# A decoder layer on one core: in its second mixing stage the four normalisations of a half stand a slot later, with one identity tile for all stages and a reordered head of the first mixing stage

## The chip, the cores and the metric

The kernel runs on one core of one Trainium2 chip. The metric is the device time of one execution in microseconds (us), as the median of three runs. Before the change it is 3562.73 us (3561.97 to 3564.03).

## The reference

Shapes are B=4 sequences of T=1024 tokens with D=512 features. Three residual blocks follow one another, each fed with a row-wise layer normalisation of x:

```python
x = x + attention(layernorm(x))             # 16 heads of 32, ALiBi distances, @ Wout + bout
x = x + mixing(layernorm(x), ctx_1024)      # below
x = x + conv_ffn(layernorm(x))              # quantised 512 -> 2048, 3-tap convolution, 2048 -> 512

def mixing(x, ctx):
    emb = x + ctx
    q, k, v = emb @ wq + bq, emb @ wk + bk, emb @ wv + bv
    ek, ew = exp(k - max_k), exp(w - max_w)             # w: pos_bias, kept within 128 of the diagonal
    y = sigmoid(q) * (ew @ (ek * v)) / (ew @ ek)
    a = layernorm(y @ wo + bo + emb) * gamma + beta
    ff = relu(a @ w1 + b1) @ w2 + b2
    return layernorm(ff + a) * gamma + beta
```

The output must be float32 of shape 4x1024x512.

## The kernel before

Six stages run one after the other, each a function with its own tiles, its own semaphores and a block in which every engine has its own program: `project_qkv`, `attend`, `mix_in` (the first mixing stage), `mix_out` (the second), `cross_ffn`, `quantised_ffn`. Between two stages all engines meet at a barrier. What one stage hands to the next goes through DRAM. A float32 product is done as three products of a high part (`_hi`, rounded by ScalarE) and a low part (`_lo`, the difference, by VectorE or GpSimd). All order is written out by hand; nothing is planned by a program. An engine works its list in order, so one that waits holds everything that stands behind it. Each stage builds its own identity tile `ident` on GpSimd (`identity`, L95: a memset and a select) for TensorE's transposes, and TensorE waits for it with `pe.wait_ge(ident_step, 2)`.

**attend.** 16 turns (a sequence by a group of four heads), each of 32 units. GpSimd starts with an iota (L662), VectorE makes `neg_distance` of it (L851), and GpSimd multiplies it into `bias_table` (L685), one head after the other; VectorE's maximum of the first unit (L863) needs the first of them. SyncE loads the stacked q and k of the turn (L649), then v.

**mix_in.** It works on eight halves of 512 tokens. Its head prepares four weights, `NAMES = ("out", "k", "v", "q")`, through the raw buffers `w_raw` (a view of `kT`): SyncE loads, `round_w` on ScalarE (L1240) rounds, `split_w` on VectorE (L1294) subtracts. The head then does, for half 0: `out_products` on TensorE (L1160, 48 matmuls of 512 columns on `o_in`), `bias_x` on GpSimd (L1113), `residual_norm` on VectorE (L1305 adds, L1307 statistics, L1311 and L113 to L118 the root, L1317 four normalisations), `embed` on GpSimd (L1121 adds the context, L1125 the bias), and TensorE's `turn` (L1189), which transposes the result. After that `step` runs for each half. In the head GpSimd and VectorE wait for all five bias vectors first, and VectorE splits the weights "out" and "k" before `residual_norm(0)`.

**mix_out.** It works on sequences b of eight tiles of 128 tokens; a *slot* s of the loop handles tile s. In the slot, TensorE does in this order: `turn_y(s-2)` (L1622), `turn_e` of a tile ahead (L1604), `weigh` for "den" (L1637 with the sums, then L1643) and for "num", `turn_e` again, and `out_product` of tile s-2 (L1666, 12 matmuls). VectorE does: `split_y(s-2)` (L1747), which `out_product` waits for; `divide(s)` (L1755, L1758, L1761); `residual(s-3)` (L1773 reads the bank of `out_product`, L1775 takes statistics). When `residual` ends a half of four tiles (slots 6 and 2), VectorE adds there the aggregation (L1780), the root (L113 to L118, fourteen small instructions) and four normalisations of 128x512 (L1787). GpSimd's `scale_and_shift` (L1559, L1561) waits for these (`norm_ready`) and stands in slots 7 and 0 for the first half, 3 and 4 for the second, behind its own `split_e` (L1551) of those slots.

There are four banks `acc`. Which one a product takes is fixed by `bank_of` and `free_bank`, and "den" of slot s takes the bank that "out" used two slots earlier:

```python
at = len(KINDS) * s + KINDS.index(kind)
back = at - ACC
before, step = KINDS[back % len(KINDS)], back // len(KINDS)
past(pe, read[before], b * TB + step - (LAG if before == "out" else 0) + 1)
```

With three kinds, `ACC` 4 and `LAG` 2 this makes "den" of slot s wait until L1773 has read output tile s-4, which VectorE does in slot s-1.

## Time and profile before

| | us |
|---|---|
| median of three runs | 3562.73 |
| the profiled execution, its device time | 3561.91 |
| its span, first to last instruction | 3560.3 |
| TensorE busy | 3177.0 (89%) |
| VectorE busy | 2358.0 (66%) |
| ScalarE busy | 1769.2 (50%) |
| GpSimd busy | 1127.6 (32%) |

Stages in time, by the first instructions of each: `attend` from 345.6, `mix_in` from 1477.4, `mix_out` from 1936.0, `cross_ffn` from 2296.6, `quantised_ffn` from about 3100. TensorE is busy nearly all the time within the stages, and idle in their heads. In the timeline a row gives start, duration, engine, line, operation, and in square brackets the idle time of the engine before it with what ended it. PE is TensorE, DVE VectorE, ACT ScalarE, POOL GpSimd, SP SyncE; an engine's name with q is its queue issuing a transfer.

### The profile page before, as it was taken

What the parts mean: (1) busy time and instruction counts of PE and PEld (TensorE: products, weight loads), DVE (VectorE), ACT (ScalarE), POOL (GpSimd) and SP (SyncE); (2) the same over time, 40 slices, a digit from 0 to 9 for tenths busy, and PEclk for the clock granted to TensorE, in tenths of its full rate; (3) what the DMA queues carried; (4) which work ended last, traced back from release to release, by engine and by line L of the source; (5) the groups of instructions that cost most, each with busy time, mean ns of one, the idle gap of its engine ahead of it and who ended that gap; (6) DMA issues with size and microseconds to landing.
All of it is one profiled execution on the core that took longest, in us unless ns stands there. A gap on an engine that the chain in (4) does not pass through costs nothing. (4 is left out here: it accounts for less than half of the span.)

```text
span 3560.3 us, 57155 instructions
## 1 busy us (share of the span) xinstructions
PE 3177.0 (89%) x19234; PEld 2286.5 (64%) x19234; DVE 2358.0 (66%) x4214; ACT 1769.2 (50%) x3131; POOL 1127.6 (32%) x892
## 2 busy tenths in 40 slices
PE   6998999999999999689996898599999999467887
PEld 5776666666666666467775777477887888334443
DVE  5562888888888888555553788634445444379996
ACT  3331888888888888412222222132222222066662
POOL 2343222311321231143331355311111111058886
PEclk9999999999999999889997999799999999689999
DMA  6775212211311222355644443321111110201112
GB/s 216 242 244 166 67 57 74 77 60 56 91 60 57 69 80 64 123 188 187 226 167 155 135 142 124 101 95 42 42 42 43 42 41 30 80 23 54 60 42 71
DMA packets 239608, 350.54 MB, mean 98 GB/s; under 512 B 31792, under 2 KB 129104, under 8 KB 239440
## 3 DMA queue, kind: packets, MB, share of 16 engines
q1 hardware_dynamic: 208784, 291.46, 25.3%
q0 software_dynamic: 8640, 31.77, 2.7%
q10 hardware_dynamic: 22016, 25.17, 2.0%
q8 instruction: 93, 1.52, 0.2%
q14 instruction: 75, 0.61, 0.1%
HBM read 210.68 MB, written 137.64 MB: 98 GB/s over the span
## 5 line engine op out<-in xcount | busy, mean ns | idle before, releaser
L863 DVE CUSTOM_DVE_ANT_0 attend_scores<-attend_scores,attend_bias_table 128x1024 f32<-128x1024 f32 x512 | 630.4, 1231 | 164.0 <-PE attend_scores L717 157.7
L790 ACT ACTIVATE attend_probs<-attend_scores,attend_neg_max 128x1024 f32<-128x1024 f32 x512 | 571.2, 1116 | 136.9 <-DVE attend_neg_max L863 126.8
L729 PE MATMUL attend_turned<-attend_ident,attend_probs 128*128 128x128 f32 x4096 | 557.5, 275 | 11.5 <-DVE attend_probsT L871 11.2
L729 PEld LDWEIGHTS attend_turned<-attend_ident,attend_probs 128*128 128x128 f32 x4096 | 473.0, 141 | 121.4 <-DVE attend_probsT L871 27.2
L717 PE MATMUL attend_scores<-attend_k_stack,attend_q_stack 96*128 96x512 f32 x1024 | 375.2, 448 | 14.4 <-DMA attend_q_stack<-qk_parts 9.8
L798 ACT COPY attend_probsT<-attend_turned 128x512 f32<-128x512 f32 x640 | 359.1, 583 | 25.4 <-PE attend_turned L729 23.5
L2207 DVE TENSOR_TENSOR cross_ffn_h_lo<-cross_ffn_hidden,cross_ffn_h_hi 128x512 fp32r<-128x512 f32 x128 | 96.3, 757 | 361.9 <-ACT cross_ffn_h_hi L2104 361.3
L691 POOL TENSOR_TENSOR attend_out_parts<-attend_out_full,attend_out_parts 128x256 fp32r<-128x256 f32 x64 | 46.5, 727 | 856.7 <-ACT attend_out_parts L805 856.7
L744 PE MATMUL attend_out_acc<-attend_probsT,attend_v_in 128*32 128x256 f32 x4096 | 312.9, 389 | 0.7 <-DVE attend_out_full L881 0.7
L871 DVE COPY attend_probsT<-attend_turned 128x512 f32<-128x512 f32 x384 | 263.4, 686 | 1.3 <-PE attend_turned L729 1.3
L717 PEld LDWEIGHTS attend_scores<-attend_k_stack,attend_q_stack 96*128 96x128 f32 x1024 | 154.1, 190 | 171.4 <-issue 169.2
L2101 ACT ACTIVATE cross_ffn_hidden<-cross_ffn_h_acc,cross_ffn_b_cols 128x512 f32<-128x512 f32 x128 | 88.1, 688 | 264.5 <-PE cross_ffn_h_acc L2018 248.5
L685 POOL TENSOR_TENSOR attend_bias_table<-attend_neg_distance,attend_slope_now 128x1920 f32<-128x1920 f32 x64 | 214.8, 3386 | 1.4 <-POOL attend_slope_now L677 0.2
L2029 PE MATMUL cross_ffn_out_acc<-cross_ffn_w_hi,cross_ffn_h_hi 128*128 128x512 f32 x512 | 206.5, 403 | 1.1 <-DVE cross_ffn_h_lo L2207 0.4
L2016 PE MATMUL cross_ffn_h_acc<-cross_ffn_aT_hi,cross_ffn_w_hi 128*128 128x512 f32 x512 | 202.8, 396 | 5.0 <-issue 4.9
L2368 POOL TENSOR_TENSOR quantised_ffn_conv<-quantised_ffn_conv,quantised_ffn_right_tap 128x512 f32<-128x512 f32 x128 | 177.7, 1388 | 89.3 <-DVE quantised_ffn_conv L2537 89.3
L2017 PE MATMUL cross_ffn_h_acc<-cross_ffn_aT_hi,cross_ffn_w_lo 128*128 128x512 f32 x512 | 202.5, 396 | 0.0
L2030 PE MATMUL cross_ffn_out_acc<-cross_ffn_w_lo,cross_ffn_h_hi 128*128 128x512 f32 x512 | 202.4, 395 | 0.0
L2104 ACT CAST cross_ffn_h_hi<-cross_ffn_hidden 128x512 fp32r<-128x512 f32 x128 | 79.4, 621 | 247.4 <-PE cross_ffn_out_acc L2031 246.4
L2031 PE MATMUL cross_ffn_out_acc<-cross_ffn_w_hi,cross_ffn_h_lo 128*128 128x512 f32 x512 | 202.3, 395 | 0.0
L2018 PE MATMUL cross_ffn_h_acc<-cross_ffn_aT_lo,cross_ffn_w_hi 128*128 128x512 f32 x512 | 202.0, 395 | 0.0
L2374 POOL TENSOR_TENSOR quantised_ffn_h_scaled<-quantised_ffn_h,quantised_ffn_scale_row 128x512 f32<-128x512 f32 x128 | 164.7, 1289 | 12.8 <-ACT quantised_ffn_scale_row L2507 8.1
(302 smaller groups left out, 6630.0 us busy)
## 6 DMA issues: line engine op xcount, KB each, us to landing
qk_parts<-qkv_qk_out SPq DMA_DIRECT2D x64, 512.0 KB, 3.2
attend_k_stack<-qk_parts SPq DMA_DIRECT2D x192, 128.0 KB, 2.5
attend_q_stack<-qk_parts SPq DMA_DIRECT2D x192, 128.0 KB, 2.6
qkv_wq_raw<-L_ffn_w POOLq DMA_DIRECT2D x16, 1024.0 KB, 7.8
o_parts<-attend_out_parts ACTq DMA_DIRECT2D x64, 256.0 KB, 2.5
mix_in_o_in<-o_parts SPq DMA_DIRECT2D x32, 512.0 KB, 6.7
qkv_x_in<-x SPq DMA_DIRECT2D x8, 1024.0 KB, 6.0
v_rows<-qkv_v_out SPq DMA_DIRECT2D x32, 256.0 KB, 3.4
```

The source lines that it names most:

```text
L685: pool.tensor_tensor(bias_table[:, h], neg_distance[:, :], slope_now[:, h:h + 1].to_broadcast([P, SPAN]), ALU.mult).then_inc(table_ready, 1)
L717: last = pe.matmul(scores[:, i % 2, k * HALF:(k + 1) * HALF], q_stack[:, h, queries], k_stack[:, h, k * HALF:(k + 1) * HALF], start=True, ...
L729: last = pe.transpose(turned[:, x, c], probs[:, i % 2, k * P:(k + 1) * P], ident[:, :])
L744: last = pe.matmul(out_acc[rows, 0:QG], v_in[:, c, rows], probsT[:, (qg - 1) % 2, c, h], start=(c == 0), stop=(c == TB - 1))
L790: act.activation(probs[:, i % 2], scores[:, i % 2], ACT.Exp, bias=neg_max[:, i % 4:i % 4 + 1], scale=-1.0, accum_out=den[:, qg % 2, j, h:h ...
L798: act.copy(probsT[:, qg % 2, x * HB:(x + 1) * HB, h, j * P:(j + 1) * P], turned[:, x]).then_inc(copied[x], 1)
L863: dve.tensor_tensor_reduce(scores[:, i % 2], scores[:, i % 2], bias_table[:, h, at:at + T], -1.0, BIG, ALU.add, ALU.min, neg_max[:, i % 4: ...
L871: dve.tensor_copy(probsT[:, qg % 2, HB:TB, h, j * P:(j + 1) * P], turned[:, 1]).then_inc(copied[1], 1)
L2016: pe.matmul(out, w1_hi[:, c, cols], aT_hi[:, c], start=c == 0, stop=False)
L2017: pe.matmul(out, w1_lo[:, c, cols], aT_hi[:, c], start=False, stop=False)
L2029: pe.matmul(out_acc[:, t], hi, w2_hi[:, j], start=j == 0, stop=False)
L2030: pe.matmul(out_acc[:, t], hi, w2_lo[:, j], start=False, stop=False)
```

## The change

There are three parts.

1. **One identity.** `ident` is made once, in `project_qkv`, kept in a tile of its own and passed to all stages; the five later copies and the waits for them go.
2. **The head of the first mixing stage.** `attend` now also loads and splits the weight "out" (`Wout`, loaded by GpSimd's queue as its first instruction of the stage, split by GpSimd after the tables of turn 0), and in its last turn loads `x_in` and `o_in` of half 0 and adds the bias to `x_in`. These five tiles live across both stages (`first`). In `mix_in` TensorE therefore starts with `out_products(0)` at once, VectorE with `residual_norm(0)`, and then splits "k", the embedding, "v" and "q"; the waits for biases are moved behind.
3. **The second mixing stage.** The four normalisations of L1787 leave `residual` and become `normalise(h)`, called after `divide(s)` of the next slot: slot 7 for the first half, slot 3 of the next sequence for the second. The last half keeps its own ending (`finish_last`).

```diff
+                def load_first():
+
+                    sp.wait_ge(wout_step, 2)
+                    sp.dma_start(first["x_in"][:, :, :], half_of(x, 0)).then_inc(x_loaded, 16)
+                    sp.wait_ge(out_stored, KB * G * 16)
+                    for g in range(KB):
+                        sp.dma_start(first["o_in"][:, g].bitcast(F32), o_parts[0, g, :, :, 0:HALF]).then_inc(first_loaded, 16)
+
                 turns(sp, body)
+                load_first()
+                sp.wait_ge(first_loaded, KB * 16)
...
+                pool.dma_start(first["x_in"][:, :, :], Wout.rearrange("(c p) n -> p c n", p=P)).then_inc(wout_loaded, 16)
+                pool.dma_start(first["bias"][:, :], row(bout, 0, D)).then_inc(wout_loaded, 16)
...
+                def split_wout():
+                    raw = first["x_in"][:, :, :]
+                    pool.wait_ge(wout_loaded, 32)
+                    pool.tensor_copy(first["w_hi"][:, :, :], raw).then_inc(wout_step, 1)
+                    pool.wait_ge(wout_step, 1)
+                    pool.tensor_tensor(first["w_lo"][:, :, :], raw, first["w_hi"][:, :, :].bitcast(F32), ALU.subtract).then_inc(wout_step, 1)
...
                     tables(turn)
...
+                    if isinstance(turn, int) and turn == 0:
+                        split_wout()
...
+                pool.wait_ge(x_loaded, 16)
+                for t in range(HT):
+                    pool.tensor_tensor(first["x_in"][:, t], first["x_in"][:, t], first["bias"][:, :], ALU.add).then_inc(x_biased, 1)
                 low_part(TURNS, 0)
                 low_part(TURNS, 1)
+                pool.wait_ge(x_biased, HT)
...
-                sp.wait_ge(o_loaded, KB * 16)
                 load_ctx(0)
-                for i, m in enumerate(NAMES[1:], 1):
-                    past(sp, w_lo_ready, i - 1)
-                    sp.dma_start(w_raw[:, i % 2], SOURCES[m].rearrange("(c p) n -> p c n", p=P)).then_inc(w_loaded[i % 2], 16)
+                def load_w(i):
+                    past(sp, w_lo_ready, i - 2)
+                    sp.dma_start(w_raw[:, i % 2], SOURCES[NAMES[i]].rearrange("(c p) n -> p c n", p=P)).then_inc(w_loaded[i % 2], 16)
+
+                load_w(1)
+                load_w(2)
                 load(1, 0, 1)
+                load_w(3)
                 store(0)
...
-                pool.wait_ge(biases_loaded, 5 * 16)
 
                 def bias_x(n):
-                    pool.wait_ge(x_loaded, (n + 1) * 16)
+                    pool.wait_ge(x_loaded, n * 16)
                     for t in range(HT):
                         pool.tensor_tensor(x_in[:, t], x_in[:, t], bias_out[:, :], ALU.add).then_inc(x_biased, 1)
...
-                bias_x(0)
+                pool.sem_inc(x_biased, HT)
                 embed(0)
                 steps(pool, step)
 
             @block.tensor
             def _(pe):
-                pe.wait_ge(ident_step, 2)
...
 
-                dve.wait_ge(biases_loaded, 5 * 16)
-                split_w(0, "out")
+                residual_norm(0)
                 split_w(1, "k")
-                residual_norm(0)
+                split_emb(0, 0)
                 split_w(2, "v")
-                split_emb(0, 0)
                 split_w(3, "q")
+                dve.wait_ge(biases_loaded, 4 * 16)
                 steps(dve, step)
...
-                        else:
-                            for j in range(HT):
-                                dve.tensor_scalar(z[:, h, j], z[:, h, j], moments[:, j, 0:1], rstd[:, j:j + 1],
-                                                  ALU.subtract, ALU.mult).then_inc(norm_ready, 1)
+
+                def normalise(h):
+
+                    for j in range(HT):
+                        dve.tensor_scalar(z[:, h, j], z[:, h, j], moments[:, j, 0:1], rstd[:, j:j + 1],
+                                          ALU.subtract, ALU.mult).then_inc(norm_ready, 1)
...
                         divide(b, s)
+                        if s == HT + LAG + 1:
+                            normalise(0)
+                        if s == LAG + 1 and not first:
+                            normalise(1)
                         if more and s == TB - 1:
                             split_sums(b + 1)
                         if not (first and s <= LAG):
...
+        project_qkv(nc, ident, x, attn_Wqkv, attn_bqkv, w1, w2, qk_parts, v_rows, w1T_parts, w2T_parts, w_mean)
+        with ExitStack() as carried:
+            sb, _, _ = memory(nc, carried, "carried", own=False)
+            first = dict(w_hi=sb("wout_hi", [P, KB, D], F32R), w_lo=sb("wout_lo", [P, KB, D], F32R),
+                         o_in=sb("o_in", [P, KB, 2, HALF], F32R), x_in=sb("x_in", [P, HT, D]), bias=sb("bias_out", [P, D]))
+            attend(nc, ident, qk_parts, v_rows, o_parts, rows(x), attn_Wout, attn_bout, first)
+            mix_in(nc, ident, rows(x), rows(ctx_1024), o_parts, first, wq, bq, wk, bk, wv, bv, bo,
+                   x1_rows, emb_rows, expq_rows, ek_cols, ekv_cols, sum_cols, pos_bias, ewT_parts, e0_rows)
```

In the order of instructions the third part shows on VectorE, in the slots 2 and 3 of the second mixing stage: the end of the root of slot 2 and then slot 3. Before:

```order
L118 SCALAR_TENSOR_TENSOR mix_out_rstd<-mix_out_nt_square,mix_out_rstd 128x4
L112 REGISTER_ALU
L1787 TENSOR_SCALAR mix_out_z<-mix_out_z,mix_out_moments,mix_out_rstd 128x512 x4
L1747 TENSOR_TENSOR mix_out_yT_lo<-mix_out_turned,mix_out_yT_hi 128x512
L1754 REGISTER_ALU
L1755 SCALAR_TENSOR_TENSOR mix_out_recip<-mix_out_expq_in,mix_out_acc 128x512
L1758 RECIPROCAL mix_out_recip<-mix_out_recip 128x512
L1761 TENSOR_TENSOR mix_out_y<-mix_out_acc,mix_out_recip 128x512
L72 REGISTER_ALU
L1773 TENSOR_TENSOR mix_out_z<-mix_out_acc,mix_out_emb_in 128x512
```

and now, with line numbers of the changed kernel:

```order
L119 SCALAR_TENSOR_TENSOR mix_out_rstd<-mix_out_nt_square,mix_out_rstd 128x4
L113 REGISTER_ALU
L1761 TENSOR_TENSOR mix_out_yT_lo<-mix_out_turned,mix_out_yT_hi 128x512
L1768 REGISTER_ALU
L1769 SCALAR_TENSOR_TENSOR mix_out_recip<-mix_out_expq_in,mix_out_acc 128x512
L1772 RECIPROCAL mix_out_recip<-mix_out_recip 128x512
L1775 TENSOR_TENSOR mix_out_y<-mix_out_acc,mix_out_recip 128x512
L1803 TENSOR_SCALAR mix_out_z<-mix_out_z,mix_out_moments,mix_out_rstd 128x512 x4
L73 REGISTER_ALU
L1787 TENSOR_TENSOR mix_out_z<-mix_out_acc,mix_out_emb_in 128x512
```

The group of four has moved from ahead of `split_y` (yT_lo) to ahead of the add that reads the bank of `out_product` (the last row). The same holds for slots 6 and 7.

SyncE's transfers from the end of `attend` into the head of `mix_in`, before:

```order
L655 DMA attend_v_in<-v_rows 128x128 x8
L637 UNCONDITIONAL_BRANCH
L1018 UNCONDITIONAL_BRANCH
L1054 DMA mix_in_kT<-L_attn_Wout 128x4x512
L1024 DMA mix_in_o_in<-o_parts 128x2x512 x4
L1027 DMA mix_in_x_in<-x 128x4x512
L1031 DMA mix_in_ctx_in<-ctx 128x4x512
L1060 DMA mix_in_kT<-L_xattn_wk 128x4x512
L1060 DMA mix_in_kT<-L_xattn_wv 128x4x512
L1060 DMA mix_in_kT<-L_xattn_wq 128x4x512
```

and now (`carried_` is the prefix of the tiles that live across both stages):

```order
L656 DMA attend_v_in<-v_rows 128x128 x8
L662 DMA carried_x_in<-x 128x4x512
L665 DMA carried_o_in<-o_parts 128x2x512 x4
L638 UNCONDITIONAL_BRANCH
L1039 UNCONDITIONAL_BRANCH
L1052 DMA mix_in_ctx_in<-ctx 128x4x512
L1078 DMA mix_in_kT<-L_xattn_wk 128x4x512
L1078 DMA mix_in_kT<-L_xattn_wv 128x4x512
L1045 DMA carried_o_in<-o_parts 128x2x512 x4
L1048 DMA carried_x_in<-x 128x4x512
L1078 DMA mix_in_kT<-L_xattn_wq 128x4x512
```

`x_in` and `o_in` of half 0 have moved ahead of the stage's border, and "q" behind the loads of half 1.

## Rows read from the trace of the kernel before

**Rows 1.** The page's first line.

```profile
span 3560.3 us, 57155 instructions
```

**Rows 2.** Waits of TensorE, whole span: total us, times, longest.

```profile
PE mix_out_acc L1666 <- DVE mix_out_yT_lo L1747: 24.7, 9, 4.9
PE mix_out_turned L1604 <- DMA mix_out_cols_in<-ekv_cols: 23.7, 1, 23.7
...
PE mix_out_acc L1637 <- DVE mix_out_z L1773: 7.6, 6, 1.4
```

**Rows 3.** Timeline of the head of `mix_in`.

```profile
1477.38 0.38 SPq L1054 DMA_DIRECT2D mix_in_kT<-L_attn_Wout  x1
...
1477.88 0.60 POOL L1103 DMA_DIRECT2D mix_in_bias_out<-L_attn_bout  x1 [4.36 <-POOLq L58]
...
1493.44 0.76 PE L1160 MATMUL mix_in_acc<-mix_in_wout_hi,mix_in_o_in 128*128 128x512 f32 x1 [22.10 <-DMA mix_in_o_in<-o_parts]
...
1510.24 0.67 DVE L1305 TENSOR_TENSOR mix_in_x<-mix_in_acc,mix_in_x_in 128x512 f32<-128x512 f32 x1
...
1514.96 3.81 DVE L1317 TENSOR_SCALAR mix_in_emb<-mix_in_x,mix_in_moments,mix_in_rstd 128x512 f32<-128x512 f32 x4
1515.65 7.50 POOL L1121 TENSOR_TENSOR mix_in_emb<-mix_in_emb,mix_in_ctx_in 128x512 f32<-128x512 f32 x4 [14.49 <-DVE mix_in_emb L1317]
...
1523.21 1.97 PE L1189 MATMUL mix_in_turned<-mix_in_ident,mix_in_emb 128*128 128x128 f32 x8 [17.01 <-POOL mix_in_emb L1121]
```

**Rows 4.** A stretch of that head: length, busy of each engine (instructions), clock, DMA.

```profile
1493.00:1507.00 14.00, 12.76 (x48) 9.97 (x48) 2.90 (x3) 3.81 (x2) 5.04 (x4) 0.88 0.76 277
```

**Rows 5.** Timeline of the head of `attend`.

```profile
347.37 2.16 DVE L851 SCALAR_TENSOR_TENSOR attend_neg_distance<-attend_offsets 128x1920 f32<-128x1920 int32 x1 [5.31 <-POOL attend_offsets L662]
...
350.42 6.73 POOL L685 TENSOR_TENSOR attend_bias_table<-attend_neg_distance,attend_slope_now 128x1920 f32<-128x1920 f32 x2
...
351.09 2.04 PE L717 MATMUL attend_scores<-attend_k_stack,attend_q_stack 96*128 96x512 f32 x4 [9.77 <-DMA attend_q_stack<-qk_parts]
...
354.04 1.23 DVE L863 CUSTOM_DVE_ANT_0 attend_scores<-attend_scores,attend_bias_table 128x1024 f32<-128x1024 f32 x1 [4.51 <-POOL attend_bias_table L685]
```

**Rows 6.** A stretch of that head, columns as in Rows 4, DMA share and GB/s last.

```profile
351.00:357.00 6.00, 2.33 (x5) 1.48 (x6) 2.47 (x4) 1.64 (x3) 6.00 (x2) 0.50 1.05 234
```

**Rows 7.** Timeline of `mix_out`, second half of a sequence, slots 2 to 4.

```profile
2063.52 1.92 DVE L1787 TENSOR_SCALAR mix_out_z<-mix_out_z,mix_out_moments,mix_out_rstd 128x512 f32<-128x512 f32 x4
...
2066.09 0.50 PE L1666 MATMUL mix_out_acc<-mix_out_w_hi,mix_out_yT_hi 128*128 128x512 f32 x1 [1.59 <-DVE mix_out_yT_lo L1747]
...
2070.66 0.68 DVE L1773 TENSOR_TENSOR mix_out_z<-mix_out_acc,mix_out_emb_in 128x512 f32<-128x512 f32 x1
...
2071.39 0.50 PE L1637 MATMUL mix_out_acc<-mix_out_sums,mix_out_e_stack 96*128 96x512 f32 x1 [1.37 <-DVE mix_out_z L1773]
```

**Rows 8.** Timeline of `mix_out`, first half of a sequence, slots 6 to 0.

```profile
2102.04 3.85 DVE L1787 TENSOR_SCALAR mix_out_z<-mix_out_z,mix_out_moments,mix_out_rstd 128x512 f32<-128x512 f32 x4
...
2106.53 0.50 PE L1666 MATMUL mix_out_acc<-mix_out_w_hi,mix_out_yT_hi 128*128 128x512 f32 x1 [3.98 <-DVE mix_out_yT_lo L1747]
...
2112.54 0.69 DVE L1773 TENSOR_TENSOR mix_out_z<-mix_out_acc,mix_out_emb_in 128x512 f32<-128x512 f32 x1
...
2113.47 0.47 PE L1637 MATMUL mix_out_acc<-mix_out_sums,mix_out_e_stack 96*128 96x512 f32 x1 [1.45 <-DVE mix_out_z L1773]
```

**Rows 9.** Twelve matmuls of `out_product` (L1666): length, PE and PEld busy, clock, DMA.

```profile
2065.00:2070.00 5.00, 3.06 (x12) 2.17 (x12) 1.00 0.00 0
2025.00:2033.00 8.00, 5.32 (x12) 3.80 (x12) 0.57 0.01 2
2104.00:2112.00 8.00, 4.62 (x12) 3.31 (x12) 0.79 0.00 1
```

**Rows 10.** Timeline of `mix_out`, first half of the last sequence.

```profile
2259.39 3.80 DVE L1787 TENSOR_SCALAR mix_out_z<-mix_out_z,mix_out_moments,mix_out_rstd 128x512 f32<-128x512 f32 x4
...
2260.02 1.49 POOL L1559 TENSOR_TENSOR mix_out_z<-mix_out_z,mix_out_gamma_row 128x512 f32<-128x512 f32 x1 [12.93 <-DVE mix_out_z L1787]
```

More of the change, by code:

```diff
@@ L42, with memory @@
 RSQRT_SEED = float(0x5F3759DF)
-def memory(nc, ctx, stage):
+def memory(nc, ctx, stage, own=True):
     def sb(name, shape, dt=F32):
@@ L58, in clear_semaphores @@
         nc.all_engine_barrier()
-    ctx.callback(clear_semaphores)
+    if own:
+        ctx.callback(clear_semaphores)
     def sem(name):
@@ L538, in _, with attend @@
                 pair(B - 1, True, False)
-def attend(nc, qk_parts, v_rows, o_parts):
+def attend(nc, ident, qk_parts, v_rows, o_parts, x, Wout, bout, first):
     GH = P // DH
@@ L664, in _ @@
                     pool.memset(slopes[:, h // GH, h % GH:h % GH + 1], SLOPE ** h).then_inc(setup_step, 1)
-                identity(pool, ident[:, :], ident_step)
                 pool.wait_ge(setup_step, HEADS)
@@ L925, in mix_in @@
         NAMES = ("out", "k", "v", "q")
-        SOURCES = dict(out=Wout, k=wk, v=wv, q=wq)
-        w_hi = {m: sb(f"w{m}_hi", [P, KB, D], F32R) for m in NAMES}
-        w_lo = {m: sb(f"w{m}_lo", [P, KB, D], F32R) for m in NAMES}
-        bias_out = sb("bias_out", [P, D])
+        SOURCES = dict(k=wk, v=wv, q=wq)
+        w_hi = {m: sb(f"w{m}_hi", [P, KB, D], F32R) for m in NAMES[1:]}
+        w_lo = {m: sb(f"w{m}_lo", [P, KB, D], F32R) for m in NAMES[1:]}
+        w_hi["out"], w_lo["out"] = first_in["w_hi"], first_in["w_lo"]
+        o_in, x_in, bias_out = first_in["o_in"], first_in["x_in"], first_in["bias"]
         bias_o = sb("bias_o", [P, D])
@@ L933, in mix_in @@
         bias_v = sb("bias_v", [P, KB])
-        ident = sb("ident", [P, P])
-        o_in = sb("o_in", [P, KB, 2, HALF], F32R)
-        x_in = sb("x_in", [P, HT, D])
         ctx_in = sb("ctx_in", [P, HT, D])
@@ L1101, in _ @@
             def _(pool):
-                for tile, vector in ((bias_out, bout), (bias_o, bo), (bias_q, bq)):
+                for tile, vector in ((bias_o, bo), (bias_q, bq)):
                     pool.dma_start(tile[:, :], row(vector, 0, D)).then_inc(biases_loaded, 16)
@@ L1121, in embed @@
                         pool.tensor_tensor(emb[:, t], emb[:, t], ctx_in[:, t], ALU.add).then_inc(emb_ready, 1)
+                    if isinstance(n, int) and n == 0:
+                        pool.wait_ge(biases_loaded, 4 * 16)
                     for t in range(HT):
@@ L1173, in out_products @@
                 def out_products(n):
-                    pe.wait_ge(o_loaded, (n + 1) * KB * 16)
+                    past(pe, o_loaded, n * KB * 16)
                     for t in range(HT):
@@ L1238, in round_w @@
                 def round_w(i, m):
-                    act.wait_ge(w_loaded[i % 2], (i // 2 + 1) * 16)
+                    act.wait_ge(w_loaded[i % 2], (i + 1) // 2 * 16)
                     act.copy(w_hi[m][:, :, :], w_raw[:, i % 2]).then_inc(w_hi_ready, 1)
-                for i in range(3):
+                for i in range(1, 3):
                     round_w(i, NAMES[i])
-                act.wait_ge(biases_loaded, 5 * 16)
                 def round_emb(n, h):
@@ L2359, in _ @@
                     pool.memset(y[:, 1, s, HALF + 1:], 0.0).then_inc(const_step, 1)
-                identity(pool, ident[:, :], ident_step)
                 pool.wait_ge(small_loaded, 32)
@@ L2627, in decoder_layer @@
     with ExitStack() as ctx:
+        ident = ctx.enter_context(nc.sbuf_tensor("ident", [P, P], F32))
         w_mean = ctx.enter_context(nc.sbuf_tensor("w_mean", [P, 2], F32))[:, :]
[L2629 to L2635 removed]
+        project_qkv(nc, ident, x, attn_Wqkv, attn_bqkv, w1, w2, qk_parts, v_rows, w1T_parts, w2T_parts, w_mean)
[6 more added lines that the diff above has]
+                   x1_rows, emb_rows, expq_rows, ek_cols, ekv_cols, sum_cols, pos_bias, ewT_parts, e0_rows)
+        mix_out(nc, ident, ewT_parts, e0_rows, wo, gamma, beta, emb_rows, expq_rows, ek_cols, ekv_cols, sum_cols, a_rows)
+        cross_ffn(nc, ident, xw1, xb1, xw2, xb2, gamma, beta, a_rows, x1_rows, w_mean, x2_rows, xq_parts, x_units)
+        quantised_ffn(nc, ident, w1T_parts, conv_w, conv_b, w2T_parts, w_mean, x2_rows, xq_parts, x_units, rows(out))
 INPUTS = ["x", "ctx_1024", "L0_attn_Wqkv", "L0_attn_bqkv", "L0_attn_Wout", "L0_attn_bout",
```

51 lines of the change are left out of this document (13 added, 38 removed).

## The prediction

> **What bounds the kernel now.** I read the page first: 3560.3 us of span [rows 1], with TensorE busy for nine tenths of it. So what counts is TensorE's idle time. The chain of waits shows it in two kinds that this change touches. In each stage's head TensorE waits once for long; within `mix_out` it waits nine times for `split_y` (24.7 us) and six times for `residual`'s add (7.6 us) [rows 2]. The timelines then give the order of events at these places: the head of `mix_in` [rows 3], the head of `attend` [rows 5], and `mix_out` around the end of a half [rows 7, 8, 10]. There the reader is to see one thing. VectorE works from the root to the add without a gap, and TensorE waits for it at two points of its list, `out_product` (L1666) and the next slot's "den" (L1637). The last view is a table of stretches: the same twelve matmuls take 3.06 us where the granted clock is 1.00, that is 2.4 GHz, and 4.62 or 5.32 us after TensorE had waited about 4 us and the clock had dropped to the level of 1.2 GHz [rows 9].
>
> **One identity.** The GpSimd work removed is a memset and a select per stage. In `mix_out` TensorE waits 23.7 us for its first columns, by a DMA, whatever the identity does [rows 2]; `mix_in`'s head likewise waits for `o_in` [rows 3], and the other heads behave alike. I count nothing. If that cover went, two such small instructions are well under 1 us per stage.
>
> **The head of `mix_in`.** Before, the stage's first transfer is issued at 1477.38 and TensorE starts at 1493.44, when `o_in` lands [rows 3]. The 48 matmuls take 12.76 us [rows 4], to 1506.20. VectorE is then behind, since it has split two weights: its last add starts at 1510.24, the normalisations 4.72 us later at 1514.96, GpSimd's four adds run 1515.65 to 1523.15, TensorE transposes from 1523.21 [rows 3]. After, weights and `o_in` are there. TensorE starts at the border: I take 1477.9 (the first GpSimd row of the stage, 1477.88 [rows 3]). It ends 12.8 us later, 1490.7. An add with its statistics is shorter than the quarter of 12.8 us that a tile's products need, so VectorE follows, and its last add starts at 1490.75. Then the unchanged pieces: 4.72 to the normalisations (1495.5), 8.19 from there to the last context add (1523.15 less 1514.96), so the transposes start at 1503.7. That is 19.5 us earlier. VectorE's long weight split still follows directly on the normalisations ("k" in place of "v"), so I keep GpSimd's 7.50 us as it is. What could be late next: context, "k" and "v" are now 3 MB issued first, where before "out", `o_in` and `x_in`, 4 MB, had been; the context has 18 us. "q" is issued only after the split of "k", near 1502.6, and is wanted by ScalarE about 1509, when the half's rounding is done: tight, but VectorE's next step waits later still, for the band. All after the head shifts as a whole, nothing here waits for a fixed time. Term: -19.5, between -18.5 and -20.5.
>
> **The head of `attend`.** GpSimd issues two transfers ahead of its iota, at about 0.60 us each [rows 3]. VectorE's distance then starts some 1.2 us later than 347.37. The tables follow it (before, 0.9 us after its end), and the first maximum waits for a table [rows 5]. The identity removed stood between them beside VectorE's distance and gives nothing back. So +1.15 at least. "Out" also brings 1 MB plus a broadcast bias of 0.25 MB into a stretch in which the DMA engines are full, at 234 GB/s [rows 6]: 5.4 us of their time, ahead of or among the first q and k, which TensorE gets at 351.09 [rows 5]. The first maximum has 0.9 us of slack for that (score ready 353.13, start 354.04); an estimate is that later heads have more. Upper bound 5.4 less 0.9, 4.5. I take +2.0, nearer the lower end. GpSimd's split of "out" and its bias adds lie where it is idle for most of a turn; the 3 MB of `x_in` and `o_in` go out in the last turn, tens of us before they are wanted. These cost nothing; without that cover GpSimd's four adds would be 5 us.
>
> **`mix_out`, second half of a sequence (three times).** After the root ends at 2063.52, before: normalisations 1.92, split, TensorE's `out_product` at 2066.09 after a wait of 1.59, `divide`, add at 2070.66, "den" at 2071.39 after a wait of 1.37 [rows 7]. After: the split goes first, 2063.52 to 2064.2. TensorE, ready at 2064.50, doesn't wait, and that 1.59 is gone. But the normalisations now stand between `divide` and the add. The add is what "den" of the next slot waits for. VectorE has had no gap, so the sum of its work up to the add is the same, and the add would end at the same time, if the four took 1.92 us again. I don't think they do. GpSimd is idle by then and waits for exactly these four; where it does so now, it starts 0.63 us into them and they take 3.80 us [rows 10], and in `mix_in` the same, 3.81 [rows 3]. At 2063.52 GpSimd was not at its scaling and they took 1.92 [rows 7]. So the add ends 1.9 us later, "den" starts at 2073.3 in place of 2071.39, and TensorE, which arrives at 2068.4, has waited 4.9 us in one piece.
>
> The Trainium skill speaks against this part of the change: "SBUF — State Buffer", section "Who interferes with whom", has VectorE in such a mode and GpSimd exclude each other for whole instructions, whichever issues first, and names tensor_scalar among those that can be in it. That is what the two kinds of row show, 1.92 us alone and 3.80 us against GpSimd. With the rule the sum is as here; were it not to hold in the new place, the sum would be 5.7 us less.
>
> **`mix_out`, first half (four times).** Here the four were already contended, 3.85 us from 2102.04; `out_product` waits 3.98, the add is at 2112.54, "den" at 2113.47 [rows 8]. After: split at 2102.04, `out_product` at 2102.8 after 0.2 in place of 3.98, done at 2105.9; `divide` to 2107.4; normalisations to 2111.2; add at 2112.5. The same time, as VectorE's gapless list has the same sum. TensorE arrives at 2106.7 and waits 6.8 us. Nothing gained: the wait has moved from `out_product` to "den" and joined the one there. (Arrival: the 12 matmuls, then 0.87 us of transposes, as from 2106.53 + 4.62 to 2113.47 - 1.45.) The last sequence's first half ends alike; there it is the split of the next tile that stands behind the normalisations, and TensorE's last products wait for it.
>
> **The clock.** This is the part that costs. Before, TensorE's clock fell after its waits of about 4 us and not after 1.59; the twelve matmuls after took 4.62 and 5.32 where 3.06 is usual: 1.6 to 2.3 us lost [rows 9]. In the first halves that loss was free, since TensorE then waited 1.45 for the add anyway. After the change all seven long waits (4.9 or 6.8 us) end at the add, and behind them TensorE alone sets the pace, VectorE having gaps. So each costs its slow stretch in full. I take 1.8, near the lower row, as the shorter loss occurs more often. Term: 7 x 1.8 = 12.6 plus 3 x 1.9 = 5.7, together +18.3; bounds 7 x 1.2 + 5.7 = 14.1 and 7 x 2.3 + 5.7 = 21.8.
>
> **The sum.** -19.5 + 2.0 + 18.3 = +0.8. The profiled execution took 3561.91 us, 0.8 below the median of the three runs. 3561.91 + 0.8 = 3562.7; I forecast 3563.0. With the bounds: -20.5 + 1.15 + 14.1 = -5.3 and -18.5 + 4.5 + 21.8 = +7.8, so 3556.6 to 3569.7. 0.2% is 7.1 us, about what a measurement of this kernel tells from no change.
>
> **Rivals.**
> - *The moved waits are cheap* (0.20). The normalisations run at 1.92 us, or the clock recovers sooner than in rows 9. For: GpSimd's arrival shifts with the slot. Against: it is idle and waiting. With +5 in `mix_out`: -19.5 + 2 + 5 = -12.5, 3549.4.
> - *The waits go and don't come back* (0.07). TensorE's "den" isn't held by the add. Then the seven waits at `out_product` (most of the 24.7 us [rows 2]) fall away: -19.5 + 2 - 22 = -39.5, 3522. Against: the waits of 1.37 and 1.45 for that very add [rows 7, 8].
> - *The clock stays low longer* (0.08, slower). One mechanism: after a wait of 6.8 us the slow stretch reaches past the first dozen matmuls. At 3.0 us a stall `mix_out` costs 26.7 and the time is 3571. It decides from 2.7 us a stall on, where the sum passes +7.1; the longest of rows 9 cost 2.3.
> - *The head isn't won* (0.05, slower). TensorE is held at the border or by its first transposes, as "q", the context or GpSimd come late. With half of the 19.5: 3572.
> - Forecast as worked out: 0.60.
>
> **How the numbers follow.** Faster by over 0.2%: the first two rivals, 0.27. Slower: the next two, 0.13. Within: 0.60. The range holds the forecast's own 3556.6 to 3569.7 and reaches to the cheap-waits rival below and to 3571 above, as more than 2 in 10 would be left out otherwise: 3547 to 3571.
>
> **What would show it.** In the changed profile: TensorE's first row of `mix_in` within 1 us of the first transfer, and its transposes 26 us after that (1523.2 less 1477.4 was 46). In `mix_out` the waits for `split_y` down to those of the last tiles, one of them near 6.8 us, and those for the add up from 7.6 to about 35 us, three of 4.9 and three of 6.8. The four normalisations at 3.8 us in all seven halves. In stretches from each "den" on, a clock below 1.00 for a few us. `attend` starting its first maximum 1 to 4.5 us later. It is wrong if "den" starts soon after `out_product`, if the normalisations take 1.9 us, or if the clock holds through the long waits.

## The result, and the profile after

The changed kernel took 3570.96 us (median of 14 runs, 3565.08 to 3574.37), the kernel before 3562.06 (14 runs). The ratio is 1.0023, with a 95% interval from 1.0015 to 1.0031: some 8 us slower. The interval lies above 1, and it holds the 1.002 that the prediction took as its border between "within" and "slower". I had forecast 3563.0, in a range of 3547 to 3571. The profiled execution took 3569.78 us, and its page begins with this row, which answers to [rows 1]:

```profile
span 3568.2 us, 57145 instructions
```

The span is 7.9 us longer, and that is a sum over stages. The first DMA issue of a tile gives each stage's start. Here are the issues of four tiles in the kernel before (the shortest, median and longest issue in ns, then first and last start in us); the start of `mix_in` is 1477.38 [rows 3]:

```profile
L649 SPq DMA_DIRECT2D attend_k_stack<-qk_parts x192: 310/316/427, 345.6 to 1392.6; - x192
...
L1492 SPq DMA_DIRECT2D mix_out_cols_in<-ek_cols x32: 378/388/1450, 1936.0 to 2208.6; - x32
...
L1929 SPq DMA_DIRECT2D cross_ffn_a_in<-a_rows x8: 367/406/512, 2296.1 to 2874.7; - x8
```

And the same in the changed kernel:

```profile
L650 SPq DMA_DIRECT2D attend_k_stack<-qk_parts x192: 310/316/1272, 343.3 to 1393.3; - x192
...
L1052 SPq DMA_DIRECT2D mix_in_ctx_in<-ctx x8: 382/433/434, 1479.2 to 1799.4; - x8
...
L1508 SPq DMA_DIRECT2D mix_out_cols_in<-ek_cols x32: 378/384/1297, 1926.0 to 2210.4; - x32
...
L1947 SPq DMA_DIRECT2D cross_ffn_a_in<-a_rows x8: 368/405/508, 2303.1 to 2883.2; - x8
```

Differences of neighbouring starts are the lengths of the stages, in us:

| stage | before | after | difference | forecast |
|---|---|---|---|---|
| up to `attend` | 345.6 | 343.3 | -2.3 | 0 |
| `attend` | 1131.8 | 1135.9 | +4.1 | +2.0 |
| `mix_in` | 458.6 | 446.8 | -11.8 | -19.5 |
| `mix_out` | 360.1 | 377.1 | +17.0 | +18.3 |
| the rest | 1264.2 | 1265.1 | +0.9 | 0 |

The row that is off is `mix_in`. (The first row varies by itself. In the changed kernel and the runs below that have its `attend` the start lies between 343.3 and 347.9, so I read no gain into the 2.3.)

The waits of TensorE in the changed kernel (total us, times, longest), which answer to [rows 2]:

```profile
PE mix_out_acc L1651 <- DVE mix_out_z L1787: 35.2, 6, 6.7
...
PE attend_scores L741 <- DMA attend_q_stack<-qk_parts: 15.3, 1, 15.3
...
PE mix_out_acc L1680 <- DVE mix_out_yT_lo L1761: 10.3, 6, 6.8
PE mix_in_acc L1181 <- DVE mix_in_x L1324: 8.7, 3, 6.7
```

In `mix_out` it is the forecast picture. The waits for the add (L1651, for z) grew from 7.6 to 35.2 us, those for `split_y` fell from 24.7 to 10.3. The fourth row is one that I had not forecast, a wait of 6.7 us in `mix_in`.

**The head of `mix_in`.** Timeline (start, length, engine), which answers to [rows 3]:

```profile
1479.29 0.76 PE L1181 MATMUL mix_in_acc<-carried_wout_hi,carried_o_in 128*128 128x512 f32 x1 [6.30 <-PEq L58]
...
1497.45 3.81 DVE L1336 TENSOR_SCALAR mix_in_emb<-mix_in_x,mix_in_moments,mix_in_rstd 128x512 f32<-128x512 f32 x4
...
1498.15 7.49 POOL L1141 TENSOR_TENSOR mix_in_emb<-mix_in_emb,mix_in_ctx_in 128x512 f32<-128x512 f32 x4 [15.80 <-DVE mix_in_emb L1336]
...
1505.69 1.54 PE L1210 MATMUL mix_in_turned<-ident,mix_in_emb 128*128 128x128 f32 x6 [13.11 <-POOL mix_in_emb L1141]
```

TensorE starts 0.05 us after the first transfer, and the transposes come 26.4 us after it (1505.69 less 1479.24), where they came 45.8 us after it before. So 19.4 us are won here.

**Behind the head.** Some 20 us later 7.3 of them are gone again:

```profile
1504.54 0.37 SPq L1078 DMA_DIRECT2D mix_in_kT<-L_xattn_wq  x1
1504.96 0.50 SPq L1056 DMA_DIRECT2D x_rows<-mix_in_x  x1
1506.89 11.80 SPq L1059 DMA_DIRECT2D emb_rows<-mix_in_emb_bo  x4
...
1514.38 3.94 POOL L1147 TENSOR_TENSOR mix_in_emb_bo<-mix_in_emb,mix_in_bias_o 128x512 f32<-128x512 f32 x2 [6.30 <-DMA emb_rows<-mix_in_emb_bo]
...
1525.87 0.55 DVE L1350 TENSOR_REDUCE mix_in_band_max<-mix_in_band 128x1 f32<-128x384 f32 x1 [9.94 <-POOL mix_in_band L1156]
...
1528.30 0.77 PE L1181 MATMUL mix_in_acc<-mix_in_eT_hi,mix_in_wk_hi 128*128 128x512 f32 x1 [6.70 <-DVE mix_in_x L1324]
```

SyncE's queue holds the load of the q weight until k is split, and behind it in the queue stands the store of x1. Both go out within half a microsecond, 1504.54 and 1504.96, 1 MB each. The first store of an `emb_bo` tile, 0.25 MB, is issued at 1506.89 and frees its buffer for GpSimd at 1514.38, 7.5 us later. In the kernel before, GpSimd waited 0.96 us at the same place:

```profile
1526.56 2.51 POOL L1125 TENSOR_TENSOR mix_in_emb_bo<-mix_in_emb,mix_in_bias_o 128x512 f32<-128x512 f32 x2 [0.96 <-DMA emb_rows<-mix_in_emb_bo]
```

All that stands in line behind it is late by the same amount: the next context and the band on SyncE, the band's mask and the bias of x on GpSimd, the maximum of the band and x1's add on VectorE, and at last TensorE's first products for k, 6.70 us. From the first transposes of one half to the first of the next (two starts in the timeline) it is 50.9 us before (1523.21 to 1574.11) and 58.2 after (1505.69 to 1563.93).

**The second half of a sequence in `mix_out`**, slot 3, which answers to [rows 7]:

```profile
2058.89 3.80 DVE L1803 TENSOR_SCALAR mix_out_z<-mix_out_z,mix_out_moments,mix_out_rstd 128x512 f32<-128x512 f32 x4
...
2059.51 1.50 POOL L1574 TENSOR_TENSOR mix_out_z<-mix_out_z,mix_out_gamma_row 128x512 f32<-128x512 f32 x1 [2.43 <-DVE mix_out_z L1803]
...
2062.61 0.68 DVE L1787 TENSOR_TENSOR mix_out_z<-mix_out_acc,mix_out_emb_in 128x512 f32<-128x512 f32 x1
...
2063.34 0.79 PE L1651 MATMUL mix_out_acc<-mix_out_sums,mix_out_e_stack 96*128 96x512 f32 x1 [5.08 <-DVE mix_out_z L1787]
```

The four normalisations, 1.92 us here before, take 3.80 with GpSimd starting 0.6 us into them, the add stands behind them, and TensorE waits 5.08 us for the add.

### The profile page after: what moved, and what is told of

Read it like the earlier page. It is cut to its first block and busy times, and to the rows that moved or that the text cites. A ratio compares the mean times of both kernels' runs of the same rounds, so it can differ in the third digit from the quotient of the medians.

```text
span 3568.2 us, 57145 instructions
## 1 busy us (share of the span) xinstructions
PE 3178.2 (89%) x19234; PEld 2291.3 (64%) x19234; DVE 2362.5 (66%) x4213; ACT 1767.1 (50%) x3130; POOL 1134.7 (32%) x885
## 5 line engine op out<-in xcount | busy, mean ns | idle before, releaser
L753 PE MATMUL attend_turned<-ident,attend_probs 128*128 128x128 f32 x4096 | 557.3, 275 | 12.6 <-DVE attend_probsT L895 12.5
L753 PEld LDWEIGHTS attend_turned<-ident,attend_probs 128*128 128x128 f32 x4096 | 472.8, 140 | 121.3 <-DVE attend_probsT L895 30.2
```

Source lines behind the costliest of these rows:

```text
L753: last = pe.transpose(turned[:, x, c], probs[:, i % 2, k * P:(k + 1) * P], ident[:, :])
```

## The experiments

All ratios are to the kernel before. The changed kernel's own is 1.0023, so a difference of 0.0010 between two ratios is 3.6 us. The intervals are 0.0008 to 0.0015 to either side, so a difference of two ratios is known to some 4 us only, and to 6 or 7 where both kernels were timed few times. Stage lengths are differences of the same starts as above, from the profiled execution.

**The move alone.** The kernel before, with the part of the diff that concerns `normalise` in `mix_out`.

> The kernel before with the later normalisations in mix_out alone. Theory (the move costs what mix_out grew by in the changed kernel, 360.1 to 377.1 us, and nothing else helps or hurts it): mix_out 377 us, time 3562 + 17 = 3579, ratio 1.0048. Rival (a shifted mix_in in the changed kernel is what disturbed mix_out): mix_out under 367 us, time 3562 to 3569.

Measured: 3581.95 us, ratio 1.0054 (1.0040 to 1.0067). `mix_out` took 377.4 us, and its waits are those of the changed kernel, 35.2 us for the add. The move costs 17 us whatever stands ahead of it.

**All but the move.** The changed kernel, with the normalisations back in `residual`.

> The changed kernel with mix_out's normalisations back in the slot of the root; the one identity and the reordered head stay. Theory (of the 19.4 us won in mix_in's head 7.5 are lost again before the first keys' products, attend costs 1.9): mix_in 446.7 us, mix_out 360, time 3562 - 9 = 3553, ratio 0.9975. Rival (my forecast's terms for the head, -19.5 and +2.0, and the loss behind the head is an accident of the one profiled execution): 3544.5, ratio 0.995.

Measured: 3553.07 us, ratio 0.9969 (0.9957 to 0.9981), `mix_in` 446.0, `mix_out` 359.7. The loss behind the head is no accident of one execution: GpSimd's wait for the `emb` store is 6.3 us here too.

**The q weight early.** It is loaded into a view of the still unused `vT`, right behind v.

```diff
+        q_raw = vT[:, :, :].rearrange("p (i a) (b n) -> p i (a b) n", i=2, n=D)[:, 0]
...
                 load_w(2)
+                sp.dma_start(q_raw, SOURCES["q"].rearrange("(c p) n -> p c n", p=P)).then_inc(q_loaded, 16)
                 load(1, 0, 1)
-                load_w(3)
...
```

ScalarE and VectorE then read `q_raw` where they read `w_raw` for q.

> The changed kernel, but the raw q weight is loaded into the still unused vT right behind the raw v, without a wait for the split of k. So no 1 MB transfer stands ahead of the x1 and emb stores. Theory (that transfer delays the emb stores, these the next context and the band): GpSimd waits about 1 us for the emb stores instead of 6.3, the first keys' products come 7 us earlier against the stage's start, time 3571 - 7.5 = 3563.5, ratio to before 1.0004. Rival (the stores are slow in themselves, or the band's load is late by SyncE's order): GpSimd's wait stays over 5 us and the time at 3571, ratio 1.0023.

Measured: 3563.78 us, ratio 1.0000 (0.9991 to 1.0009), which is 8 us less than the changed kernel; `mix_in` took 435.3 us. Its timeline at the same place:

```profile
1501.36 0.38 SPq L1058 DMA_DIRECT2D x_rows<-mix_in_x  x1
1506.97 5.04 SPq L1061 DMA_DIRECT2D emb_rows<-mix_in_emb_bo  x4
...
1509.13 2.52 POOL L1149 TENSOR_TENSOR mix_in_emb_bo<-mix_in_emb,mix_in_bias_o 128x512 f32<-128x512 f32 x2 [0.96 <-DMA emb_rows<-mix_in_emb_bo]
```

The `emb` store is issued at the same time as in the changed kernel (1506.97 and 1506.89, with transposes at 1505.8 and 1505.7), but frees its buffer 2.2 us later, not 7.5. The x1 store had gone out at 1501.36, 3.6 us earlier than in the changed kernel. So the cause is the q load at that place. Of the 11.5 us by which `mix_in` is shorter in this profile, 8.5 lie between the first half's transposes and the second's (49.77 us, 58.24 in the changed kernel). Another 1.6 lie in a later half, where the clock fell in the changed kernel's profile (0.83 over 10 us) and not in this one (1.00). Below, two profiles of the same code show how this comes and goes. This run takes away two things at once, the q's megabyte ahead of the small store and the wait that held the x1 store back until right in front of it; which of the two costs more it does not tell.

**The wait in `mix_out` filled.**

```diff
                         if not (first and s < LAG):
                             out_product(b, s)
+                        if s == 3 and not first:
+                            for k in range(18):
+                                pe.matmul(sum_acc[:, 0], w_hi[:, 0, 0:P], w_hi[:, 1], start=True, stop=True)
```

> The changed kernel, but TensorE makes 18 products more, into a bank that nobody reads at this time, at the end of the fourth slot of the second, third and fourth sequences: 18 times 0.23 is 4.1 us, inside a wait of 5 us. Their result is not used. Theory (the dropped clock behind the wait costs about 2 us each time, at 0.43 us a product instead of 0.23): the den and num products behind the three waits keep 0.23 us each, mix_out 3 x 1.9 = 5.7 us shorter (371.4), time 3565. Rival (what counts is the wait itself, the slow products are hidden by VectorE's reciprocal): mix_out 377, time 3571.

Measured: 3565.87 us, ratio 1.0007 (0.9998 to 1.0016). The granted clock of three stretches of this run, the fillers, "den" and "num" (busy time with the count, clock, DMA share, GB/s), TensorE alone:

```profile
2061.00:2065.09 4.09, 4.09 (x19) 1.00 0.00 0
2067.16:2069.60 2.44, 2.44 (x10) 1.00 0.55 141
2069.60:2071.93 2.33, 2.33 (x11) 1.00 0.94 274
```

And of the changed kernel, "den" right behind its wait of 5.08 us, and then "num":

```profile
2063.34:2067.60 4.26, 4.26 (x10) 0.51 0.69 188
2067.67:2070.00 2.33, 2.33 (x12) 1.00 0.26 98
```

With TensorE busy until 1.04 us before the add is there, the clock stays at 1.00, 2.4 GHz; with a wait of 5.08 us it comes back at 0.51, near the level of 1.2 GHz, and the first ten products take 4.26 us in place of 2.44. Behind them it is at 1.00 again. That is 1.8 us a stall, and it is on the path, since VectorE's `divide` waits for "den" behind it, 3.26 us in the changed kernel and 1.37 with the wait filled:

```profile
2067.87 0.69 DVE L1769 SCALAR_TENSOR_TENSOR mix_out_recip<-mix_out_expq_in,mix_out_acc 128x512 f32<-128x512 f32 x1 [3.26 <-PE mix_out_acc L1657]
```

```profile
2067.16 0.50 PE L1651 MATMUL mix_out_acc<-mix_out_sums,mix_out_e_stack 96*128 96x512 f32 x1 [1.04 <-DVE mix_out_z L1790]
...
2069.80 0.69 DVE L1772 SCALAR_TENSOR_TENSOR mix_out_recip<-mix_out_expq_in,mix_out_acc 128x512 f32<-128x512 f32 x1 [1.37 <-PE mix_out_acc L1657]
```

Here the first fence is the changed kernel's timeline and the second that of this run. From the first four normalisations to the last it is 248.5 us (92.1 to 340.6 after the stage's start) against 254.1 (90.4 to 344.5) in the changed kernel, 5.6 less for three stalls. The whole stage is only 2.5 us shorter in this profile, 374.6, since its start and end were some 3 us longer; the ratios say 5.7, known to some 4. So the rival, that VectorE hides the slow products, is out.

**Behind the add.** The calls of `normalise` moved down, in the same slots.

```diff
                         divide(b, s)
-                        if s == HT + LAG + 1:
-                            normalise(0)
-                        if s == LAG + 1 and not first:
-                            normalise(1)
                         if more and s == TB - 1:
                             split_sums(b + 1)
                         if not (first and s <= LAG):
                             residual(b, s - LAG - 1)
+                        if s == HT + LAG + 1:
+                            normalise(0)
+                        if s == LAG + 1 and not first:
+                            normalise(1)
```

> The changed kernel, with the four normalisations called behind the slot's add instead of ahead of it. Theory (TensorE's den is held by that add, and the normalisations ahead of it are what made the wait long): the waits for z fall from 35.2 us to under 12, those for split_y grow by less than 5, the clock falls less often, mix_out 350 us or less in place of 377.1, time 3571 - 27 = 3544. Rival (VectorE has no slack there either, and what is won at the add comes back at the next split_y): the waits for yT_lo grow from 10.3 to over 30 us, mix_out over 368, time 3562 or more.

Measured: 3547.46 us, ratio 0.9960 (0.9946 to 0.9973). `mix_out` took 358.3 us, 18.8 less than changed and 1.8 less than before. The waits:

```profile
PE mix_out_acc L1651 <- DVE mix_out_z L1787: 19.4, 11, 3.0
...
PE mix_out_acc L1680 <- DVE mix_out_yT_lo L1761: 11.3, 7, 6.8
```

The direction holds, and what was won doesn't come back at `split_y`. But I had expected under 12 us of waits for the add and 350 us for the stage. The lateness of VectorE, from the root on, is now spread over eleven waits of at most 3.0 us instead of six of up to 6.7. The list of VectorE has not become shorter, since the four still take 3.8 us there. And the clock, which I had expected to fall less often, still falls at some of the first halves. Here is TensorE in the 6 us behind the waits of 3.00, 1.37, 3.00 and 2.81 us (columns as above):

```profile
2020.26:2026.26 6.00, 6.00 (x21) 0.72 0.61 177
2058.39:2064.39 6.00, 5.99 (x28) 1.00 0.64 175
2098.32:2104.32 6.00, 5.03 (x23) 1.00 0.61 175
2176.22:2182.22 6.00, 6.00 (x14) 0.50 0.57 178
```

Behind all eight waits of 1.0 to 1.4 us it is at 1.00; behind the three of 2.8 to 3.0 us it is 0.72, 1.00 and 0.50. At the first of them the fall comes 1.2 us after the wait has ended.

**GpSimd's scaling a slot later.**

```diff
-                        if s == 0 and not first:
-                            scale_and_shift(b - 1, 0, range(2, HT))
-                        if s in (3, 4) and not first:
-                            scale_and_shift(b - 1, 1, range(2 * (s - 3), 2 * (s - 2)))
+                        if s in (0, 1) and not first:
+                            scale_and_shift(b - 1, 0, range(2 * s, 2 * s + 2))
+                        if s in (4, 5) and not first:
+                            scale_and_shift(b - 1, 1, range(2 * (s - 4), 2 * (s - 3)))
...
-                        if s == 7:
-                            scale_and_shift(b, 0, range(2))
...
```

> The changed kernel, with GpSimd's scaling of a half a slot later too (slots 0 and 1, 4 and 5 of the next sequence's eight), so that it is not working against the normalisations. Theory (the 3.80 us are contention with GpSimd's scaling): the four take 1.92 us in all seven places, the waits for z are 1.9 us shorter each (three of 3, three of 4.9), mix_out 13 us shorter (364), and up to 6 more if the clock doesn't fall behind a wait of 3 us; time 3552 to 3558. Rival (the normalisations are slow for another reason in the new place, such as the products writing PSUM beside them): 3.8 us stays, time 3571.

Measured: 3564.09 us, ratio 1.0002 (0.9993 to 1.0011), `mix_out` 373.7. Less than expected, 7.5 us by the ratios and 3.4 by the stage, and the timeline says why:

```profile
2058.17 2.85 DVE L1801 TENSOR_SCALAR mix_out_z<-mix_out_z,mix_out_moments,mix_out_rstd 128x512 f32<-128x512 f32 x4
...
2058.93 1.35 POOL L1566 TENSOR_TENSOR mix_out_e_lo<-mix_out_e_full,mix_out_e_hi 128x512 fp32r<-128x512 f32 x1 [2.56 <-ACT mix_out_e_hi L1713]
```

GpSimd's scaling is gone from this place, but one of its splits of e now falls into it. The four take 2.85 us, between 1.92 with GpSimd idle and 3.80 with it working from 0.6 us on. The waits for the add are still 4.1 to 5.8 us, and even behind one of 4.14 us the first ten products come at the level of 1.2 GHz:

```profile
2061.67:2065.97 4.30, 4.30 (x10) 0.50 0.71 213
```

**Wout late.** The two loads that GpSimd issues ahead of its iota stand behind the tables of turn 0 instead.

> The changed kernel, with the loads of Wout and its bias issued by GpSimd behind the first turn's tables instead of ahead of its iota. Theory (attend's head is later because 1.25 MB stand ahead of the first q and k, and because of the two issues): TensorE's first scores come 5.5 us after the stage's first transfer, as before, not 10 to 11; attend is 2.5 us shorter, time 3568.5. Rival (the head's lateness is caught up or has another cause): the first scores stay at 10 us, or they come early and the time stays at 3571.

Measured: 3565.87 us, ratio 1.0014 (1.0005 to 1.0023). `attend` took 1132.1 us, as long as before the change, and its first scores come 5.2 us after the first transfer, as the timeline shows with the first transfer at 345.24:

```profile
350.42 2.08 PE L741 MATMUL attend_scores<-attend_k_stack,attend_q_stack 96*128 96x512 f32 x4 [9.44 <-DMA attend_q_stack<-qk_parts]
```

In the changed kernel it was 11.1 us (343.33 to 354.39). The ratio alone can't tell the two kernels apart (3.2 us, less than the intervals allow). The stage lengths can: over the profiles, `attend` took 1134.2 to 1134.7 us in the six experiments with the early load of Wout, and 1132.1 to 1132.3 in the four with the late one. So the early load's price is 2.2 us, and the changed kernel's own profile, with 1135.9, is the highest of its kind. (With the old `attend` it was 1131.8 twice and, with the one identity alone, 1129.2.)

**The early q without the move.**

> The reordered head of mix_in with the early q, without the later normalisations in mix_out. Theory (the parts add up): 3571 - 17.5 for mix_out - 7.5 for the q, 3546, ratio 0.9955. Rival (the two parts gain against the same wait and don't add up): 3553, no better than without the early q.

Measured: 3543.97 us, ratio 0.9950 (0.9936 to 0.9964), `mix_in` 433.1, `mix_out` 359.3. The parts add up.

**One identity alone.** The kernel before with the identity made once.

> The kernel before with one identity for all stages and nothing else. Theory (the two small GpSimd instructions of a stage lie under a DMA wait): same time, ratio 1.000 with 0.001 to either side. Rival (a stage's head is shorter by them, or the carried tile's place in memory matters): 2 us or more to either side.

Measured: 3561.31 us, ratio 0.9996 (0.9987 to 1.0005). It is worth nothing that can be told.

**The complete head.** Early q, late Wout, `mix_out` as before.

> Head of mix_in with the early q, Wout's load behind the first turn's tables, mix_out as before. Theory (the parts add up, the late Wout gives attend's 2.5 us back): 3544 - 2.5 = 3541.5, ratio 0.9944. Rival (the late Wout's split delays GpSimd's next tables or the q): 3544 or more.

Measured: 3542.20 us, ratio 0.9943 (0.9929 to 0.9956), as expected.

**The complete head, with the normalisations behind the add.**

> As the run with the complete head, but with mix_out's normalisations behind the next slot's add. Theory (mix_out took 358.3 us in that form and 359.3 as before): 3540, ratio 0.994, level with the complete head alone within 2 us. Rival (the form is worth more where the clock falls less often): 3535 or less.

Measured: 3540.63 us, ratio 0.9940 (0.9926 to 0.9954), `mix_out` 356.7. Its `mix_in` took 439.8 us, 3.6 more than the run before it (436.2) with the same code there. The clock accounts for 3.2 of these. From one half's first transposes to the next half's it is 50.5 us in this run at two of the seven steps, the second and the sixth, and 48.9 in the run before at the same two. Here are the first 10 us of the second step, first this run and then the run before, TensorE alone:

```profile
1556.60:1566.60 10.00, 8.14 (x38) 0.83 0.08 28
```

```profile
1554.50:1564.50 10.00, 8.14 (x45) 1.00 0.08 28
```

TensorE is busy for the same 8.14 us of the stretch in both, with one wait of 1.86 us in it. In one execution the granted clock is 1.00, in the other it is 0.83 and seven matmuls fewer fit in. What decides it isn't shown.

**And GpSimd's scaling later.** The last run's kernel with the diff of the scaling on top.

> As the run before (complete head, normalisations behind the add), with GpSimd's scaling a slot later too. Theory (a product of GpSimd inside the four normalisations costs VectorE about 0.95 us, and with the scaling a slot later there is at most one of them, as 2.85 us in place of 3.80 showed): 7 x 0.95 us less in VectorE's list, of which TensorE waits for a part: mix_out 353 to 356, time 3536, ratio 0.993. Rival (behind the add VectorE has the slack to hide it): 3540, no difference.

Measured: 3528.74 us (4 runs, 3525.74 to 3533.44), ratio 0.9910 (0.9895 to 0.9925), the fastest of all. `mix_out` took 348.2 us. The four normalisations of a first half, and the waits for the add:

```profile
2005.27 1.90 DVE L1803 TENSOR_SCALAR mix_out_z<-mix_out_z,mix_out_moments,mix_out_rstd 128x512 f32<-128x512 f32 x4
```

```profile
PE mix_out_acc L1651 <- DVE mix_out_z L1787: 12.9, 6, 3.0
```

More than expected. Behind the add no split of e falls into the four of the first three sequences' first halves, so they take 1.90 us. Those of the second halves take 2.3 to 2.4, and only the last sequence's first half still takes 3.8. VectorE's list is 1.4 to 1.9 us shorter in six of the seven halves, and the stage 8.5 us shorter than with the scaling in its old place. `mix_in` is 4.2 us shorter too (435.6) with the same code, 3.2 of them since both steps take 48.9 us again. So of the 12 us between the two medians the scaling is shown to be worth the stage's 8.5.

## Why the forecast held, and where it failed

- **The number: in the range by luck.** 3570.96 us is inside it by 0.04 us. The forecast's own bounds ended at 3569.7; the range went on to 3571 for a rival, the clock that stays low longer, which did not happen. The slowdown of 0.23% is also just past the border of 0.2%, on the side to which I had given 0.13, and its interval has both sides of the border.
- **The head of `mix_in`, up to the transposes: right.** 19.4 us won, 19.5 forecast, by the steps given.
- **"All after the head shifts as a whole, nothing here waits for a fixed time": wrong.** This is the step that failed. I had looked at whether q comes in time for those who want it ("tight, but VectorE's next step waits later still, for the band"), and not at what its issue holds back and what its megabyte delays. It stands in SyncE's queue ahead of the x1 store, the `emb` stores, the context and the band. 7.3 us went back, and with q moved away (ratio 1.0023 to 1.0000) they are won. `mix_in` then takes 433.1 to 436.2 us in four of the five runs with the early q, 22 to 26 less than before, and 439.8 in the fifth. The surplus over 19.5 lies in the steps between transposes. In the profile of "The q weight early" the first step is 1.1 us shorter than before (49.8 us against 50.9) and the second 1.9 (48.9 against 50.8), with a granted clock of 1.00 in place of 0.83 in its first 10 us; the fourth and sixth are shorter by 0.9 and 0.8, for which I have no cause. The clock's part comes and goes with the same code.
- **The head of `attend`, +2.0: right in size.** 2.2 by the runs with the late Wout; the +4.1 of the table is the changed kernel's one profile. Of the two causes that I gave, the DMA's is the one that counts. The first maximum starts 12.5 us after the stage's first transfer, 4.0 later than before; it waits for TensorE (6.73 us in its row), whose scores wait for q, and no longer for a table. So 4.0 us at the head become 2.2 over the stage.
- **`mix_out`, +18.3: right, and by the mechanism given.** 17.0 in the changed kernel, 17.3 alone. The waits at "den" sum to 35.2 us with a longest of 6.7, where I had 35 and 6.8. The normalisations took 3.8 us in all seven halves. The filled wait gives the clock's share, 1.8 us a stall (forecast 1.8), and the two runs with the scaling later show that GpSimd's work inside the four is what they pay for: 1.90, 2.85 and 3.80 us as GpSimd does nothing, one product or several. These rows agree with the rule of the Trainium skill's "SBUF — State Buffer", section "Who interferes with whom", in the new place too.
- **One identity, 0: right.**
- **The rivals.** Cheap waits (3.80 us and 0.51), vanishing waits (35.2 us at the add) and a clock that stays low longer (1.00 again from "num" on) are each excluded by the numbers above. "The head isn't won" gave 3572 by half of the 19.5 being lost, as "q", the context or GpSimd come late. It described nearly what happened in size, but at another place: TensorE was not held at the border or at its first transposes, and q was in time for its own readers. The forecast's centre is 8 us too low, and 7.3 of these are that step.

## What to carry to other kernels

When a load is moved in a queue, ask not only who waits for its data but what its issue holds back behind it and which small transfers come right after its bytes: a 0.25 MB store behind 2 MB cost its waiter 5 us and the kernel some 8. When lateness of an engine can't be removed, order its list so that what the other engine waits for comes first: the same four instructions cost 17 us ahead of the add and nothing behind it. And look at what the third engine does in the new place, since it can make the moved instructions twice as long. Last, before a stage's length in one profile is read as a gain, compare it with another execution of the same code: here two of them differ by 3.6 us, 3.2 of it by the clock.

## What the runs showed of the hardware

- A store of 0.25 MB freed its buffer 2.2 us after its issue with the last large transfer issued 5.6 us before it, and 7.5 us after it with 2 MB issued within the 2.4 us before. The Trainium skill's "DMA: Bandwidth & Descriptors", section "Queues, rings and completion order", has each DMA engine consume what one issuing engine gives it in the order of a ring, without a promise that it completes in that order. The two numbers agree with a store that is served behind the 2 MB.
- The price of GpSimd beside VectorE's four `tensor_scalar` is graded: 1.90 us with it idle, 2.85 with one instruction of 1.35 us inside, 3.80 with two whole ones inside and the start of a third.
- Eighteen products that nobody needs made the kernel some 5.7 us faster (ratio 1.0023 to 1.0007, with a difference known to some 4 us), since the clock was 1.00 behind them and 0.51 behind the bare wait.
- The granted clock behind the same code and the same wait isn't the same each time. It was 0.72, 1.00 and 0.50 behind three waits of 2.8 to 3.0 us in one run, and 0.83 in one execution and 1.00 in another over the same 10 us of `mix_in`, at 1.6 us a fall.
